# A rank update stacked on chip for the first batch, and other edits at the edges of a conditioned residual layer

## The chip, the cores and the metric

One core of a Trainium2 chip runs the kernel. The metric is the device time in microseconds, the median of several runs. Times inside a profile are microseconds from the first instruction of one profiled execution.

## The reference

For each of 32 batches, x is 512 rows by 512 features, and f is 512 features by rank 16, used on both sides:

```
z1 = einsum('bfi,bir->bfr', x, f) / 512
z  = einsum('bfr,bor->bfo', z1, f) / 16
y  = einsum('bfi,oi->bfo', x, W) + fc_bias + z + cond
out = x + gelu(y, approximate=False)
```

All of it is fp32. Since z = x (f f^T) / 8192, the layer of batch b is x times one matrix of its own, full_w = W + f f^T / 8192.

## The kernel before

Everything is held transposed: features on partitions in four chunks of 128, rows along the free dimension. For each batch TensorE forms the update f f^T in PSUM (`update`), VectorE adds it, scaled, to the base weights (`full_w`, L335), and TensorE multiplies full_w with x.

fp32 precision comes from splits. ScalarE copies a tile to the shorter fp32r type (`w_high`, L263; `x_high`, L257), VectorE subtracts that from the whole (`w_low`, `x_low`, L331), and three products are summed in PSUM: high with high, high with low, low with high. The factors are split the same way, for four batches (a group) at a time: `f_parts` holds 64 rows, 16 for each batch, as high, low and whole. From it SP copies five pieces by DMA (`stack_factors`, L175) into `f_stack`: high, high, low, low on one side against high, low, high, low on the other, 16 rows each, so that one product over 64 rows gives the update with all four terms. From batch 2 on the stack is written twice, on rows 0 to 63 and 64 to 127, and products over 64 rows are put alternately on the two halves of the array (`halves`, L457, 96 products of a batch), four phases of two output tiles each. Batches 0 and 31 use whole 128-row products (`piece` L481, and the end of `step` L576). Batch 1's update uses rows 0 to 63 only (`in_whole`, L163). `f_stack` has two buffers, used by odd and by even batches.

Batch 0 is special (`piecewise`, L127). Its factors are loaded straight to the last 16 of 128 rows of `f_first`, the other rows being zeroed, and its update is four full-precision fp32 products (`first_update`, L518): two before the first piece and one after each of the next groups of four. It is then worked off chunk by chunk: update, full_w, splits, products. Batch 1's update is put into PE's queue inside batch 0's third piece (L513), and batch 2's update at the head of batch 1's step (L568). The order on every engine is the order of the program text.

SP's queue issues all DMAs in one order: the factors of batch 0, x and weights in chunks, the factors of group 0, x of batch 1, the biases; then, behind a wait for the split factors of group 0, stack 1 (five DMAs), the factors of all other groups in one load of 896 KB, stack 2 (ten DMAs), x of batch 2. In the step of batch b it issues stack b + 3 after the update of batch b + 1, in the first step also x of batch 3, then the two stores of the batch, then x of batch b + 4. ScalarE in step b takes the last GELUs of batch b - 1, the splits of batch b + 1, the first GELUs of b. A half product of a new batch waits until the GELU has read its bank.

The last batch finishes its four output tiles one after another; the last tile is one GELU, one addition of x and one store, both stores of it by SP.

## Time and profile before

| what | us |
| --- | --- |
| three runs | 380.54, 381.37, 382.89 (median 381.37) |
| profiled execution, its time | 380.12 |
| its span, first to last instruction | 378.3 |
| PE busy | 371.0 (98%) |
| DVE (VectorE) busy | 296.7 (78%) |
| ACT (ScalarE) busy | 203.8 (54%) |
| chain that ended last | PE 93%, SP's queue 3%, DMA 2%, DVE 1% |
| granted TensorE clock | 1.000 over the span |

The chain that ended last is followed back from the last instruction, at each step to what released it. PE is TensorE's products, PEld its weight loads, SPq the issuing of DMAs by SyncE. The time "to landing" of a DMA runs from its issue. Matmuls are pipelined, so their records overlap, and a name of a line can be that of a helper.

### The profile page before, as it was taken

To read this page: it belongs to the slowest core of one execution; us is meant where nothing else is said; L and a number is where in the kernel's file an instruction comes from. 1 tells how busy PE (TensorE), PEld (TensorE's weight loads), DVE (VectorE), ACT (ScalarE), POOL (GpSimd) and SP (SyncE) were. 2 spreads that over 40 slices of the span, in tenths; PEclk is the share of its full clock that TensorE was granted. 3 is DMA by queue.
4 is the path that set the end of the run, shared out by engine and by line. 5 is a ranking of instruction groups with operands and counts; after the bars stand their busy time and mean duration, and the time that the engine had idled before them with its cause. 6 is when DMAs were issued, how large, how long until landed. Compare 5 with 4: busy or idle time off the path is not lost.

```text
span 378.3 us, 7900 instructions
## 1 busy us (share of the span) xinstructions
PE 371.0 (98%) x3111; PEld 302.0 (80%) x3111; DVE 296.7 (78%) x182; ACT 203.8 (54%) x209; POOL 0.7 (0%) x5
## 2 busy tenths in 40 slices
PE   8989999999999999999999999999999999999995
PEld 4768888888888888888888888888888888888874
DVE  5699788887788877788877878878778987778932
ACT  5385445665455565545565446575445665446531
POOL 0000000000000000000000000000000000000000
PEclk9999999999999999999999999999999999999999
DMA  7999887678786778787678886777887777883222
GB/s 242 258 248 334 280 269 230 204 234 246 217 267 223 204 233 243 220 264 231 194 231 246 233 251 229 204 233 236 241 244 233 202 235 231 244 243 124 113 113 112
DMA packets 27565, 85.50 MB, mean 226 GB/s; under 512 B 6752, under 2 KB 6880, under 8 KB 23584
## 3 DMA queue, kind: packets, MB, share of 16 engines
q1 hardware_dynamic: 27552, 85.32, 73.5%
q8 instruction: 9, 0.15, 0.2%
q14 instruction: 4, 0.03, 0.0%
HBM read 35.75 MB, written 33.55 MB: 183 GB/s over the span
## 4 chain that ended last, share of the span: by engine, by line
PE 93%; SPq 3%; DMA 2%; DVE 1%; issue 0%; ACT 0%; DVEq 0%
PE y L454 86%; PE update L538 4%; SPq L186 2%; DMA f_stack<-f_parts 1%; PE y L438 1%; PE y L446 1%; PE y L442 1%; DMA base_w<-w_t 1%; DVE full_w L335 0%; SPq L206 0%; ACT result L293 0%; DVE result L385 0%; DVE f_parts L331 0%; DVE w_low L331 0%; DVE x_low L331 0%
## 5 line engine op out<-in xcount | busy, mean ns | idle before, releaser
L454 PE MATMUL y<-x_high,w_high 64*128 64x512 f32 x960 | 186.9, 386 | 0.0
L454 PE MATMUL y<-x_low,w_high 64*128 64x512 f32 x960 | 186.9, 386 | 0.0
L293 ACT ACTIVATE result<-y,bias 128x512 f32<-128x512 f32 x128 | 81.2, 686 | 159.1 <-PE y L454 151.3
L454 PE MATMUL y<-x_high,w_low 64*128 64x512 f32 x960 | 128.3, 386 | 0.0
L385 DVE TENSOR_TENSOR result<-result,x_in 128x1024 f32<-128x1024 f32 (+1 forms) x65 | 78.3, 1204 | 55.7 <-ACT result L293 55.7
L454 PEld LDWEIGHTS y<-x_low,w_high 64*128 64x128 f32 x960 | 89.9, 184 | 18.9
L454 PEld LDWEIGHTS y<-x_high,w_high 64*128 64x128 f32 x960 | 89.9, 184 | 18.9
L454 PEld LDWEIGHTS y<-x_high,w_low 64*128 64x128 f32 x960 | 89.9, 184 | 18.9
L335 DVE SCALAR_TENSOR_TENSOR full_w<-update,base_w 128x2048 f32<-128x2048 f32 (+2 forms) x36 | 73.9, 2054 | 21.6 <-PE update L538 18.6
L331 DVE TENSOR_TENSOR w_low<-full_w,w_high 128x2048 fp32r<-128x2048 f32 (+1 forms) x35 | 73.5, 2101 | 0.3
L331 DVE TENSOR_TENSOR x_low<-x_in,x_high 128x2048 fp32r<-128x2048 f32 (+1 forms) x35 | 73.5, 2100 | 0.0
L263 ACT ACTIVATE w_high<-full_w 128x2048 fp32r<-128x2048 f32 x31 | 59.4, 1915 | 4.6 <-DVE full_w L335 4.6
L257 ACT ACTIVATE x_high<-x_in 128x2048 fp32r<-128x2048 f32 x31 | 59.4, 1916 | 1.2 <-DMA x_in<-x_t 1.2
L538 PE MATMUL update<-f_stack 64*128 64x512 f32 x124 | 19.8, 389 | 1.6 <-DMA f_stack<-f_parts 1.6
L538 PEld LDWEIGHTS update<-f_stack 64*128 64x128 f32 x124 | 11.8, 184 | 4.8 <-DMA f_stack<-f_parts 2.1
L438 PE MATMUL y<-x_high,w_high 128*128 128x512 f32 x32 | 11.9, 418 | 0.0
L442 PE MATMUL y<-x_low,w_high 128*128 128x512 f32 x32 | 11.4, 403 | 0.0
L446 PE MATMUL y<-x_high,w_low 128*128 128x512 f32 x32 | 9.6, 406 | 0.0
L438 PEld LDWEIGHTS y<-x_high,w_high 128*128 128x128 f32 x32 | 6.4, 199 | 2.7 <-issue 1.4
L446 PEld LDWEIGHTS y<-x_high,w_low 128*128 128x128 f32 x32 | 5.9, 188 | 2.0 <-issue 0.6
L442 PEld LDWEIGHTS y<-x_low,w_high 128*128 128x128 f32 x32 | 6.0, 188 | 1.6 <-issue 0.5
L520 PE MATMUL update<-f_first 128*128 128x512 f32 x8 | 5.8, 843 | 0.0
(18 smaller groups left out, 22.9 us busy)
## 6 DMA issues: line engine op xcount, KB each, us to landing
out_t<-result SPq DMA_DIRECT2D x63, 512.0 KB, 3.4
x_in<-x_t SPq DMA_DIRECT2D x31, 1024.0 KB, 6.2
f_stack<-f_parts SPq DMA_DIRECT2D x183, 64.0 KB, 4.2
f_stack<-f_parts SPq DMA_DIRECT2D x122, 32.0 KB, 4.4
x_in<-x_first SPq DMA_DIRECT2D x4, 256.0 KB, 4.1
base_w<-w_t SPq DMA_DIRECT2D x4, 256.0 KB, 4.3
f_parts<-factors SPq DMA_DIRECT2D x1, 896.0 KB, 8.8
out_t<-result SPq DMA_DIRECT2D x2, 256.0 KB, 2.5
```

What stands on the lines that cost most here:

```text
L186: sp.dma_start(f_stack[slot][row + g * RANK:row + (g + 1) * RANK, sides, :].bitcast(fp32), pair).then_inc(stacked[slot], 16)
L257: nc.scalar.activation(x_high[j % SLOTS][:, :, :], x_in[j][:, :, :], ACT.Copy).then_inc(x_high_ready, 1)
L263: nc.scalar.activation(w_high[j % SLOTS][:, :, :], full_w[:, :, :], ACT.Copy).then_inc(w_high_ready, 1)
L293: nc.scalar.activation(result[j % SLOTS][:, m, :], y[m][:, :], ACT.Gelu, bias=bias[:, bass.ds(b * CHUNKS + m, 1)]).then_inc(gelu_ready, 1)
L331: nc.vector.tensor_tensor(out, whole, high.bitcast(fp32), ALU.subtract).then_inc(ready, 1)
L335: nc.vector.scalar_tensor_tensor(full_w[:, chunks, start:stop], update[:, chunks, start:stop], UPDATE_SCALE, base_w[:, chunks, start:stop] ...
L385: nc.vector.tensor_tensor(part, part, x_in[j][:, chunks, :], ALU.add).then_inc(result_ready, 1)
L438: nc.tensor.matmul(y[m][:, :], w_high[slot][:, c, m * P:(m + 1) * P], x_high[slot][:, c, :], start=(c == 0), stop=False)
L442: nc.tensor.matmul(y[m][:, :], w_high[slot][:, c, m * P:(m + 1) * P], x_low[slot][:, c, :], start=False, stop=False)
L446: mm = nc.tensor.matmul(y[m][:, :], w_low[slot][:, c, m * P:(m + 1) * P], x_high[slot][:, c, :], start=False, stop=(c == CHUNKS - 1))
L454: return nc.tensor.matmul(y[m][:, :], w[rows, c, m * P:(m + 1) * P], x[rows, c, :], start=first, stop=last)
L538: mm = nc.tensor.matmul(update[:, c, :], f_stack[slot][rows, 0, c * P:(c + 1) * P], f_stack[slot][rows, 1, :], start=True, stop=True)
```

## The change

It does the following.
- The 16 factor rows of batch 0 are loaded four times, to 64 rows (`f_first`). ScalarE makes the high part in two halves of 256 columns. VectorE makes each side of the stack as whole - high x mask, where the mask of a row is 1 on the rows that are to hold low parts; the masks come from a row number (GpSimd's iota), a bitwise and, and a multiplication. Rows 64 to 127 of both stacks are zeroed once.
- The updates of batches 0 and 1 are single fp32r products over 128 rows. The third and fourth of batch 0 now both stand behind the first group of high products.
- SP loads group 1's factors alone (128 KB), waits for batch 0's updates before stack 2 (the same buffer now holds batch 0's stack), and loads groups 2 to 7 (768 KB) in the first step, ahead of x of batch 3.
- The last output tile is finished in two halves of 256 columns; the second half is stored by ScalarE's queue.
- PE makes 8 idle products at the start instead of 3.

```diff
--- before.py
+++ after.py
@@ -31,6 +31,7 @@
 def cond_residual_kernel(nc, x_t, x_first, w_t, factors, cond, fc_bias, out_t):
     fp32 = mybir.dt.float32
     fp32r = mybir.dt.float32r
+    int32 = mybir.dt.int32
     ALU = mybir.AluOpType
     ACT = mybir.ActivationFunctionType
 
@@ -46,9 +47,12 @@
     PART_DMAS = 5
     HALF = CHUNKS // 2
     PIECEWISE = 1
-    WARM_UPS = 3
+    WARM_UPS = 8
     EDGE = FEATURES // 2
 
+
+    EDGES = [slice(n * EDGE, (n + 1) * EDGE) for n in range(2)]
+    LAST_PARTS = [(slice(CHUNKS - 1, CHUNKS), cols) for cols in EDGES]
 
     PHASES = ((0, 1), (2, 3), (1, 0), (3, 2))
 
@@ -73,7 +77,11 @@
         result = [sb(f"result{s}", [P, CHUNKS, ROWS], fp32) for s in range(SLOTS)]
 
 
-        f_first = sb("f_first", [P, FEATURES], fp32)
+        f_first = sb("f_first", [TILE, FEATURES], fp32)
+        f_first_high = sb("f_first_high", [TILE, FEATURES], fp32r)
+        rows = sb("rows", [TILE, 1], int32)
+        row_bit = sb("row_bit", [TILE, 2], int32)
+        low_rows = sb("low_rows", [TILE, 2], fp32)
         f_parts = sb("f_parts", [UNROLL * RANK, GROUPS, 3, FEATURES], fp32)
 
 
@@ -89,16 +97,22 @@
         y = [ps(f"y{m}", [P, ROWS], fp32) for m in range(CHUNKS)]
 
         f_first_loaded = sem("f_first_loaded")
-        f_first_zeroed = sem("f_first_zeroed")
+        rows_numbered = sem("rows_numbered")
+        bits_ready = sem("bits_ready")
+        low_rows_ready = sem("low_rows_ready")
+        f_first_high_ready = sem("f_first_high_ready")
+        first_moving_stacked = sem("first_moving_stacked")
+        first_weights_stacked = sem("first_weights_stacked")
         edge_full_w_ready = sem("edge_full_w_ready")
         edge_w_high_ready = sem("edge_w_high_ready")
-        f_loaded = [sem("f_loaded_group0"), sem("f_loaded_rest")]
+        f_loaded = [sem("f_loaded_group0"), sem("f_loaded_group1"), sem("f_loaded_rest")]
         bias_loaded = sem("bias_loaded")
         w_loaded = [sem(f"w_loaded{c}") for c in range(CHUNKS)]
         x_first_loaded = [sem(f"x_first_loaded{c}") for c in range(CHUNKS)]
         x_loaded = [sem(f"x_loaded{s}") for s in range(X_SLOTS)]
         f_high_ready = sem("f_high_ready")
         f_low_ready = sem("f_low_ready")
+        stack_zeroed = sem("stack_zeroed")
         stacked = [sem(f"stacked{s}") for s in range(SLOTS)]
         bias_ready = sem("bias_ready")
         idle_zeroed = sem("idle_zeroed")
@@ -168,6 +182,11 @@
             engine.dma_start(x_in[j][:, :, :],
                              batch_chunks(x_t, UNROLL * t + j, slice(0, CHUNKS))).then_inc(x_loaded[j], 16)
 
+        def store(engine, t, j, part):
+            chunks, cols = part
+            engine.dma_start(batch_chunks(out_t, UNROLL * t + j, chunks)[:, :, cols],
+                             result[j % SLOTS][:, chunks, cols]).then_inc(stored[j % SLOTS], 16)
+
         block = ctx.enter_context(nc.Block())
 
         @block.sync
@@ -190,7 +209,8 @@
             def load_first_x(c):
                 sp.dma_start(x_in[0][:, c, :], x_first[c]).then_inc(x_first_loaded[c], 16)
 
-            sp.dma_start(f_first[P - RANK:P, :], factors[0:RANK, 0, :]).then_inc(f_first_loaded, 16)
+            sp.dma_start(f_first[:, :], factors[0:RANK, 0, :].rearrange("(a r) i -> a r i", a=1)
+                         .to_broadcast([TILE // RANK, RANK, FEATURES])).then_inc(f_first_loaded, 16)
             load_first_x(0)
             sp.dma_start(base_w[:, 0, :], w_t[0]).then_inc(w_loaded[0], 16)
             sp.dma_start(f_parts[:, 0, 2, :], factors[:, 0, :]).then_inc(f_loaded[0], 16)
@@ -203,7 +223,8 @@
 
             sp.wait_ge(f_low_ready, 1)
             stack_factors(0, 1)
-            sp.dma_start(f_parts[:, 1:GROUPS, 2, :], factors[:, 1:GROUPS, :]).then_inc(f_loaded[1], 16)
+            sp.dma_start(f_parts[:, 1, 2, :], factors[:, 1, :]).then_inc(f_loaded[1], 16)
+            sp.wait_ge(update_ready, made(0))
             stack_factors(0, 2)
             load_x(sp, 0, 2)
 
@@ -217,15 +238,16 @@
                     sp.wait_ge(update_ready, made(b + 1))
                     stack_factors(t3, j3)
                 if is_first(t, j):
+                    sp.dma_start(f_parts[:, 2:GROUPS, 2, :], factors[:, 2:GROUPS, :]).then_inc(f_loaded[2], 16)
                     load_x(sp, 0, 3)
-                parts = [slice(0, HALF), slice(HALF, CHUNKS)]
+                whole_row = slice(0, ROWS)
+                parts = [(slice(0, HALF), whole_row), (slice(HALF, CHUNKS), whole_row)]
                 if is_last(t, j):
-                    parts[1:] = [slice(m, m + 1) for m in range(HALF, CHUNKS)]
+                    parts[1:] = [(slice(m, m + 1), whole_row) for m in range(HALF, CHUNKS - 1)] + [LAST_PARTS[0]]
                 for n, part in enumerate(parts):
 
                     sp.wait_ge(result_ready, 2 * b + n + 1)
-                    sp.dma_start(batch_chunks(out_t, b, part),
-                                 result[j % SLOTS][:, part, :]).then_inc(stored[j % SLOTS], 16)
+                    store(sp, t, j, part)
                 if j == 0 and not last_group:
 
                     sp.wait_ge(f_low_ready, t + 2)
@@ -236,13 +258,13 @@
             groups(sp, step)
 
             sp.wait_ge(stored[0], 2 * 16 * BATCHES // SLOTS)
-            sp.wait_ge(stored[1], 2 * 16 * BATCHES // SLOTS + 16 * (HALF - 1))
+            sp.wait_ge(stored[1], 2 * 16 * BATCHES // SLOTS + 16 * HALF)
 
         @block.scalar
         def _(act):
             def split_factors(t):
 
-                act.wait_ge(f_loaded[0 if isinstance(t, int) and t == 0 else 1], 16)
+                act.wait_ge(f_loaded[t if isinstance(t, int) and t < 2 else 2], 16)
                 nc.scalar.activation(f_parts[:, bass.ds(t, 1), 0, :].bitcast(fp32r),
                                      f_parts[:, bass.ds(t, 1), 2, :], ACT.Copy).then_inc(f_high_ready, 1)
 
@@ -290,11 +312,18 @@
                     act.wait_ge(stored[j % SLOTS], 2 * 16 * (UNROLL // SLOTS * t + j // SLOTS))
                 if m == 0 and is_first(t, j):
                     act.wait_ge(bias_ready, 1)
-                nc.scalar.activation(result[j % SLOTS][:, m, :], y[m][:, :], ACT.Gelu,
-                                     bias=bias[:, bass.ds(b * CHUNKS + m, 1)]).then_inc(gelu_ready, 1)
+                columns = [slice(0, ROWS)]
+                if is_last(t, j) and m == CHUNKS - 1:
+                    columns = [cols for _, cols in LAST_PARTS]
+                for cols in columns:
+                    nc.scalar.activation(result[j % SLOTS][:, m, cols], y[m][:, cols], ACT.Gelu,
+                                         bias=bias[:, bass.ds(b * CHUNKS + m, 1)]).then_inc(gelu_ready, 1)
 
             act.wait_ge(idle_zeroed, 1)
             nc.scalar.activation(idle_gelu[:, :], idle[:, 0:1], ACT.Gelu)
+            act.wait_ge(f_first_loaded, 16)
+            for cols in EDGES:
+                nc.scalar.activation(f_first_high[:, cols], f_first[:, cols], ACT.Copy).then_inc(f_first_high_ready, 1)
             for c in range(CHUNKS):
                 high_pieces(0, c)
                 if c == 0:
@@ -325,6 +354,9 @@
 
             groups(act, step)
 
+            act.wait_ge(result_ready, 2 * BATCHES + 2)
+            store(act, GROUPS - 1, UNROLL - 1, LAST_PARTS[1])
+
         @block.vector
         def _(dve):
             def low_part(out, whole, high, ready):
@@ -357,6 +389,8 @@
                     dve.wait_ge(w_high_ready, n - CHUNKS)
                     dve.wait_ge(w_low_ready, n - CHUNKS)
                 full_weights(one, rest, FEATURES, full_w_ready)
+                if n == 1:
+                    stack_first(0, EDGES[1], first_weights_stacked)
 
             def low_pieces(b, c):
 
@@ -366,8 +400,30 @@
                 dve.wait_ge(w_high_ready, n)
                 low_part(w_low[b][:, one, :], full_w[:, one, :], w_high[b][:, one, :], w_low_ready)
 
-            nc.vector.memset(f_first[0:TILE, :], 0.0).then_inc(f_first_zeroed, 1)
-            nc.vector.memset(f_first[TILE:P - RANK, :], 0.0).then_inc(f_first_zeroed, 1)
+            for s in range(SLOTS):
+                nc.vector.memset(f_stack[s][TILE:P, :, :].bitcast(fp32), 0.0).then_inc(stack_zeroed, 1)
+
+            dve.wait_ge(rows_numbered, 1)
+            bits = (2 * RANK, RANK)
+            for side in range(2):
+                nc.vector.tensor_scalar(row_bit[:, side:side + 1], rows[:, :], bits[side], None,
+                                        ALU.bitwise_and).then_inc(bits_ready, 1)
+            dve.wait_ge(bits_ready, 2)
+            for side in range(2):
+                nc.vector.tensor_scalar(low_rows[:, side:side + 1], row_bit[:, side:side + 1], -1.0 / bits[side], None,
+                                        ALU.mult).then_inc(low_rows_ready, 1)
+
+            def stack_first(side, cols, ready):
+
+                nc.vector.scalar_tensor_tensor(f_stack[0][0:TILE, side, cols], f_first_high[:, cols].bitcast(fp32),
+                                               low_rows[:, side:side + 1], f_first[:, cols], ALU.mult,
+                                               ALU.add).then_inc(ready, 1)
+
+            dve.wait_ge(low_rows_ready, 2)
+            for n, cols in enumerate(EDGES):
+                dve.wait_ge(f_first_high_ready, n + 1)
+                stack_first(1, cols, first_moving_stacked)
+            stack_first(0, EDGES[0], first_weights_stacked)
             for c in range(CHUNKS):
                 full_piece(0, c)
                 low_pieces(0, c)
@@ -378,11 +434,11 @@
                                     fc_sb[:, :].rearrange("p (a m) -> p a m", a=1)
                                     .to_broadcast([P, BATCHES, CHUNKS]), ALU.add).then_inc(bias_ready, 1)
 
-            def add_x(t, j, chunks):
-
-                dve.wait_ge(gelu_ready, CHUNKS * (UNROLL * t + j) + chunks.stop)
-                part = result[j % SLOTS][:, chunks, :]
-                nc.vector.tensor_tensor(part, part, x_in[j][:, chunks, :], ALU.add).then_inc(result_ready, 1)
+            def add_x(t, j, chunks, cols=slice(0, ROWS)):
+
+                dve.wait_ge(gelu_ready, CHUNKS * (UNROLL * t + j) + chunks.stop + cols.start // EDGE)
+                part = result[j % SLOTS][:, chunks, cols]
+                nc.vector.tensor_tensor(part, part, x_in[j][:, chunks, cols], ALU.add).then_inc(result_ready, 1)
 
             def finish_previous(t, j):
 
@@ -424,12 +480,15 @@
                 add_x(t, j, slice(0, HALF))
 
             groups(dve, step)
-            for m in range(HALF, CHUNKS):
+            for m in range(HALF, CHUNKS - 1):
                 add_x(GROUPS - 1, UNROLL - 1, slice(m, m + 1))
+            for chunks, cols in LAST_PARTS:
+                add_x(GROUPS - 1, UNROLL - 1, chunks, cols)
 
         @block.gpsimd
         def _(pool):
             nc.gpsimd.memset(idle[:, :], 0.0).then_inc(idle_zeroed, 1)
+            nc.gpsimd.iota(rows[:, :], [[0, 1]], base=0, channel_multiplier=1).then_inc(rows_numbered, 1)
 
         @block.tensor
         def _(pe):
@@ -504,11 +563,10 @@
                     high_high(b, m, c)
                 if n == 1:
                     first_update(2)
+                    first_update(3)
                 pe.wait_ge(x_low_ready, n)
                 for m in range(CHUNKS):
                     high_low(b, m, c)
-                if n == 1:
-                    first_update(3)
                 if n == HALF + 1:
                     rank_update(0, 1)
                 pe.wait_ge(w_low_ready, n)
@@ -517,7 +575,8 @@
 
             def first_update(c):
 
-                nc.tensor.matmul(update[:, c, :], f_first[:, c * P:(c + 1) * P], f_first[:, :],
+                pe.wait_ge(first_weights_stacked, c // HALF + 1)
+                nc.tensor.matmul(update[:, c, :], f_stack[0][:, 0, c * P:(c + 1) * P], f_stack[0][:, 1, :],
                                  start=True, stop=True).then_inc(update_ready, 1)
 
             def rank_update(t, j):
@@ -534,7 +593,7 @@
                 for c in range(CHUNKS):
                     if piecewise(t, j):
                         pe.wait_ge(full_w_ready, made(b - 2) + c + 1)
-                    rows = half_rows(0 if in_whole(t, j) else c % TILES)
+                    rows = slice(0, P) if in_whole(t, j) else half_rows(c % TILES)
                     mm = nc.tensor.matmul(update[:, c, :], f_stack[slot][rows, 0, c * P:(c + 1) * P],
                                           f_stack[slot][rows, 1, :], start=True, stop=True)
                     if piecewise(t, j) or c == CHUNKS - 1:
@@ -544,8 +603,8 @@
             for _ in range(WARM_UPS):
                 nc.tensor.matmul(y[0][:, :], idle[:, 0:P], idle[:, :], start=True, stop=True)
 
-            pe.wait_ge(f_first_zeroed, 2)
-            pe.wait_ge(f_first_loaded, 16)
+            pe.wait_ge(stack_zeroed, SLOTS)
+            pe.wait_ge(first_moving_stacked, len(EDGES))
             first_update(0)
             first_update(1)
             for c in range(CHUNKS):
```

## Rows read from the trace of the kernel before

**Rows 1.** Chain that ended last, in order of time: start us, us, what

```profile
1.67 3.17 DMA base_w<-w_t
...
17.60 4.89 DMA f_stack<-f_parts
...
22.53 0.73 PE update L538 x4
...
34.17 0.45 PE update L538 x4
34.62 10.88 PE y L454 x96
```

**Rows 2.** Timeline, first 25 us: start us, us, engine, line, tiles, shapes, count [idle before]

```profile
0.74 0.52 POOL L432 MEMSET idle<- 128x512 bf16 x1 [0.29 <-POOLq L612]
0.75 0.41 SPq L193 DMA_DIRECT2D f_first<-factors  x1
0.91 0.48 DVE L369 MEMSET f_first<- 64x512 f32 x1 [0.91 <-PEq L612]
...
1.32 1.46 PE L545 MATMUL y<-idle 128*128 128x512 bf16 x3 [1.32 <-POOL idle L432]
...
2.83 3.75 PE L520 MATMUL update<-f_first 128*128 128x512 f32 x4
...
4.94 0.76 DVE L335 SCALAR_TENSOR_TENSOR full_w<-update,base_w 128x256 f32<-128x256 f32 x2 [2.90 <-PE update L520]
...
5.40 0.42 ACT L276 ACTIVATE w_high<-full_w 128x256 fp32r<-128x256 f32 x1 [0.92 <-DVE full_w L335]
...
5.96 1.82 PE L438 MATMUL y<-x_high,w_high 128*128 128x512 f32 x4
...
7.52 3.42 SPq L186 DMA_DIRECT2D f_stack<-f_parts  x5
...
15.82 1.20 PE L538 MATMUL update<-f_stack 64*128 64x512 f32 x4
...
17.05 2.29 DVE L335 SCALAR_TENSOR_TENSOR full_w<-update,base_w 128x2048 f32<-128x2048 f32 x1 [3.12 <-PE update L538]
...
19.38 1.92 ACT L263 ACTIVATE w_high<-full_w 128x2048 fp32r<-128x2048 f32 x1 [4.58 <-DVE full_w L335]
...
21.20 2.40 ACT L293 ACTIVATE result<-y,bias 128x512 f32<-128x512 f32 x4
```

**Rows 3.** Line L186 on SP: stack 1's issues and landing, then stack 3's landing

```profile
L186 SPq DMA_DIRECT2D f_stack<-f_parts x5: 590/655/752, 7.5 to 10.3; - x5
...
DMA to landing us min/median/max: 4.9/5.5/6.1
...
DMA to landing us min/median/max: 3.0/4.5/6.2
```

**Rows 4.** DMA issues, 0 to 30 us: size each, median us to landing

```profile
f_parts<-factors SPq DMA_DIRECT2D x1, 896.0 KB, 8.8
...
f_parts<-factors SPq DMA_DIRECT2D x1, 128.0 KB, 3.1
...
f_first<-factors SPq DMA_DIRECT2D x1, 32.0 KB, 1.9
```

**Rows 5.** x of batch 3: its issue, its landing, and ScalarE's split of it

```profile
25.47 0.58 SPq L168 DMA_DIRECT2D x_in<-x_t  x1
...
DMA to landing us min/median/max: 7.0/7.0/7.0
...
35.39 1.92 ACT L257 ACTIVATE x_high<-x_in 128x2048 fp32r<-128x2048 f32 x1
```

**Rows 6.** Timeline of the tail, and the last stores' row of the DMA issues

```profile
374.00 0.69 ACT L293 ACTIVATE result<-y,bias 128x512 f32<-128x512 f32 x1 [2.03 <-PE y L446]
374.71 0.69 DVE L385 TENSOR_TENSOR result<-result,x_in 128x512 f32<-128x512 f32 x1 [2.02 <-ACT result L293]
...
out_t<-result SPq DMA_DIRECT2D x2, 256.0 KB, 2.5
```

## The prediction

> **What bounds the kernel now.** I read the page's chain of waits first, then the chain in order of time, then the timeline of the first 25 us and of the last 6, then DMA landings. The chain by engine, on the page, is nearly all PE; the chain in order of time [rows 1] says which parts are not. One batch is four update products in 0.45 us and 96 half products in 10.88, together 11.33, and this pair repeats 29 times up to 362.83 without a gap between them. Nothing in the diff touches that loop: the shapes, the order and the count of its instructions stay. So only what lies before 22.9 (batch 1's first half product) and behind 374.0 (the last product) can move the time.
>
> Before 22.9 several chains run close together, and I need the one that ends last:
> - **Stack of batch 2.** Its last DMA is issued at 17.60 and lands 4.89 us later, at 22.49; PE's update follows at 22.53 [rows 1] and the first half product at about 22.87 (22.53 + 0.73 less the overlap of a 0.39 us product).
> - **ScalarE.** Batch 1's first half products open on banks that batch 0's GELUs 0 and 1 must free. The four GELUs start at 21.20 and take 2.40 in all [rows 2], steps of 0.57 with a last one of 0.69, so the second ends at 22.46. It is level with the stack: removing the stack's lateness alone gives only 22.87 - 22.46 = 0.4 us.
> - **What sets the GELUs.** They stand behind ScalarE's split of batch 1's weights (19.38, 1.92), behind VectorE's full_w (17.05, 2.29), behind the update products of batch 1 (15.82, 1.20) [rows 2]. Call the start of those products T. Before, T = 15.82, in PE's own order; the stack that they need had landed at 10.3 + 4.9 = 15.2 [rows 3]. That is the row to look at: PE can come at most 0.6 us sooner before that stack is the wait.
>
> **The change, part by part.**
>
> *Batch 0's update in single products.* Removed: 4 full-precision products, two records each; the first two products take 3.75 us for four records from 2.83 on, about 0.9 a record, and update 0 releases full_w at 4.94 [rows 2]. The weights for it land at 1.67 + 3.17 = 4.84 [rows 1], so there is nothing to win at this point even with a free update. Added ahead of it, one after the other: the load, now 64 rows and 128 KB for 32 KB; two ScalarE copies of 256 columns; three VectorE operations of 256 columns; then the product.
> - Load: bounded by the 32 KB row's 1.9 us and the 64-row 128 KB row's 3.1 us [rows 4]; I take 2.4, since that second row also queued behind 512 KB. It starts at 0.75 [rows 2] and lands at 3.15 (2.65 to 3.85).
> - ScalarE: 0.42 each [rows 2], two in a row overlapping by 0.1 as the GELUs do: 3.6 and 3.9.
> - VectorE before it: two memsets of 64x1024; the 64x512 one took 0.48 [rows 2], so 0.48 to 0.97 each, I take 0.97, nearest by elements: 0.91 to about 3.0. The four one-column operations have no row; between 0.1 (nothing but a step) and 0.3 each, I take 0.15: 3.6. The iota on GpSimd starts at 1.26 (0.74 + 0.52) and has until 3.0; its price is also unseen, from 0.1 to unknown; the nearest row is the 0.52 memset, and that is my value: hidden.
> - VectorE's three operations: 0.38 each (0.76 for two, [rows 2]): 4.0, 4.4, 4.75.
> - PE: 8 warm-ups instead of 3. Three took 1.46 [rows 2], a step of 0.42 and 0.6 for the last, so 8 end at 1.32 + 3.4 = 4.7, just under the 4.8 at which the data is there: nothing, at most 0.1. Then one weight load and one product, 0.6: update 0 ready at 5.4, full_w at 5.45 instead of 4.94, **0.5 later**.
> - Behind it VectorE has one more operation of 0.38 ahead of batch 0's splits. So the split factors are ready 0.9 later, and SP's first stack DMA, which waits for them, starts at 8.4 instead of 7.52 [rows 2].
> - PE gains: the third and fourth first products fall from two records to one, and the first group of four high products (5.96, 1.82 for four, [rows 2]), of which the first steps at 0.42, should run at the 0.227 step of the loop (10.88/48) since PE has then been busy much longer. 1.2 GHz is 0.427 for 512 columns, 2.4 GHz 0.213. Groups of four then take 0.91. With VectorE's pieces 2 us apart (three operations of a quarter of 2.29 and a little), PE opens the third piece at 12.5 and is ready for batch 1's update eight products later, at 14.3.
>
> *So T is now set by DMA.* The five DMAs of stack 1 are issued 0.9 later and still queue behind a megabyte of x; their landing is set by the bytes ahead, not by their issue (4.9 against the 3.0 of a stack that finds the queue free, [rows 3]). 96 KB more lie ahead: between 0 (they fit where the queue is still empty at the start) and 96/195 = 0.5 us, the rate at which 896 KB landed between 15.2 and 19.8 (issued behind the five at 10.3 + 0.65, landing 8.8 later) [rows 3, 4]. I take 0.2, as most of it falls into the queue's empty start: **T = 15.4**, 0.4 sooner than before.
>
> *Batch 1's update on 128 rows.* Four products of 0.227 and a last of 0.39 are 1.07 against 1.20: 0.13 sooner. full_w at 16.5 instead of 17.05, and everything on ScalarE and VectorE behind it 0.5 sooner: second GELU done at 21.95.
>
> *Group 1's factors alone.* 768 KB leave the queue ahead of stack 2: up to 3.9 us at 195 KB/us. Then the issue is the limit: the last DMA starts at 17.60 + 0.9 less about 0.2 for the smaller load = 18.3, and lands 3.0 later (the least of the ten behind it, [rows 3]) at 21.3; with update products 21.7. That is under 21.95, by 0.25 only. The new wait for batch 0's four updates passes near 8 and SP reaches it after 12: nothing. So batch 1's half products start at 22.0 instead of 22.87: **0.85 gained**.
>
> *The rest of the factors later.* 768 KB, 3.9 us of queue, now go ahead of batch 3's x, which was issued at 25.47 and took 7.0 [rows 5]. It would land at 33 to 37; ScalarE wants it at 35.39 [rows 5] less 0.85. Landing at 37 it gives x_high at 38.9 (1.92) and x_low at 41.2 (2.29), and PE wants that at 45.1 (34.62 + 11.33 - 0.85): nothing. If the cover were gone (landing after 40.8) it would cost one for one.
>
> *The tail.* Before: GELU 374.00 + 0.69, add 374.71 + 0.69, store of 256 KB landing 2.5 after issue [rows 6]. Now half GELUs 0.42 with a step of 0.34, second half's add of 0.38 done at 375.15: 0.25 sooner. The last store is 128 KB, at the rate above up to 0.65 less, but its other half travels beside it and its rows are half as long; it also goes out by ScalarE's queue, which no row shows. Between -0.3 and 1.0 for the whole tail; I take **0.5**.
>
> Sum against the profiled execution: 380.12 - 0.85 - 0.5 = 378.8. The runs' median, 381.37, lies 1.25 above it, and the same 1.35 off it gives **380.0**.
>
> **The rivals.**
> - *The broadcast load holds up the queue.* Its source has a slowest dimension of 4 (copies), where every other load here has 16 or more. If it then used 4 of the 16 engines, those carry 32 KB each, at 195/16 = 12 KB/us for an engine 2.6 us at most. What follows on those engines lags too, but the queue is not full before 5, and that rate is one of short rows; I put 1.0 of it on stack 1: T = 16.2, second GELU 22.7, stack 2 at 22.0 or so; start gains 0.15, tail 0.5: 380.7. Nothing in the trace speaks against it, as no such load is in it. The Trainium skill, DMA: Bandwidth & Descriptors, "Why a DMA increments its semaphore by 16 and not by 1", says that the number of engines is the largest up to 16 that divides both sides' slowest dimensions, which would be 4 here; at its 27 GiB/s for an engine the lag would be 1.1 us by estimate. Chance 0.27.
> - *The iota is late (slower than before).* VectorE can't mask before it. Up to 3.0 it is free; from there update 0 slips one for one. The start has 1.5 us to spare before batch 1 begins at 22.87 again (22.87 against 21.3 to 21.7 for the stack chain), and 0.5 more from the tail: it decides from an iota that ends at about 5.0, 3.7 us long. One of 6 us would end at 7.3: 4.3 later, 2.8 over, less 0.5: 383.7. For it: GpSimd ran only memsets here. Against it: the one over 512 columns took 0.52 [rows 2]. The Trainium skill, GPSIMD Engine Reference, "Instruction dispatch", gives about 6 us for the first call of a freshly loaded kernel; no row here shows one. Chance 0.10.
> - *The moved factors hurt.* x of batch 3 after 40.8, above: 382 and more. Chance 0.05.
> - *Stack 1 lands early after all*, say because the queue serves its small packets between x's: T = 14.3, 1.1 more, but then stack 2 binds at 21.3: gain 1.2 + 0.5 and a better tail: 379.2. Chance 0.08.
> - The forecast: 0.50.
>
> **The numbers.** Within the forecast the bounds are 1.35 ± 0.7 (T 0.3, tail 0.5, stack 2 0.3); the runs of one kernel spread by 2.3 us here, so a median of a few moves by some 0.8. Reaching to the first and fourth rival: 378.4 to 381.8. About 1%, 3.8 us, is what a measurement of this kernel can tell from no change. Faster than 377.6 needs more than the whole start gives: 0.03. Slower than 385.2 needs an iota of 8 us or a broken loop: 0.04. Same: 0.93.
>
> **What would show it.** Update 0 at 5.3 to 5.6; first stack DMA at 8.2 to 8.6; batch 1's update products at 15.4, with PE waiting for f_stack before them; stack 2 landed before the second GELU ends; batch 1's first half product at 22.0, released by ScalarE's GELU; the loop unchanged at 11.33; last add at 375.15. It is wrong if the first load lands after 4, if the iota ends after 3, if PE waits in batches 2 or 3, or if the update of batch 1 starts by PE's order.

## The result, and the profile after

| | us |
| --- | --- |
| changed kernel, median of 22 runs | 383.86 (383.39 to 384.40) |
| kernel before, median of 22 runs beside them | 381.99 (380.47 to 383.63) |
| ratio | 1.0055, 95% interval 1.0043 to 1.0067 |
| changed kernel, profiled execution and its span | 383.47 and 381.7 |

Slower by 1.9 us, where 380.0 and a range of 378.4 to 381.8 had been forecast. Three single runs far outside the rest (418.66 and 764.23 us of the kernel before, 538.96 us of the kernel with the small tiles last) are left out of all ratios.

The page of the changed kernel (span; engine, busy time and share; chain by engine):

```profile
span 381.7 us, 7920 instructions
PE 371.4 (97%) x3112; PEld 304.2 (80%) x3112; DVE 299.7 (79%) x191; ACT 204.7 (54%) x212; POOL 0.8 (0%) x6
...
PE 87%; SPq 7%; DMA 4%; DVE 1%; issue 1%; ACT 0%; DVEq 0%
```

TensorE's busy time is what it was (371.0), the span 3.4 us longer. The timeline of the changed kernel's start answers [rows 2]:

```profile
0.74 0.76 SPq L212 DMA_DIRECT2D f_first<-factors  x1
1.02 0.91 DVE L404 MEMSET f_stack<- 64x1024 f32 x1 [1.02 <-PEq L671]
1.29 0.12 POOL L491 IOTA rows<- 64x1 int32 x1
...
1.32 3.59 PE L604 MATMUL y<-idle 128*128 128x512 bf16 x8 [1.32 <-POOL idle L490]
...
5.56 0.72 ACT L326 ACTIVATE f_first_high<-f_first 64x256 fp32r<-64x256 f32 x2 [3.33 <-DMA f_first<-factors]
...
6.09 1.27 DVE L418 SCALAR_TENSOR_TENSOR f_stack<-f_first_high,low_rows,f_first 64x256 fp32r<-64x256 f32 x3 [2.62 <-ACT f_first_high L326]
...
7.51 0.70 PE L579 MATMUL update<-f_stack 128*128 128x512 f32 x2 [2.60 <-DVE f_stack L418]
...
8.02 0.76 DVE L367 SCALAR_TENSOR_TENSOR full_w<-update,base_w 128x256 f32<-128x256 f32 x2 [0.65 <-PE update L579]
...
9.03 2.04 PE L497 MATMUL y<-x_high,w_high 128*128 128x512 f32 x4 [0.82 <-ACT w_high L298]
...
10.99 3.35 SPq L205 DMA_DIRECT2D f_stack<-f_parts  x5
...
18.38 1.10 PE L597 MATMUL update<-f_stack 128*128 128x512 f32 x4
...
23.66 2.40 ACT L319 ACTIVATE result<-y,bias 128x512 f32<-128x512 f32 x4
```

Read down the starts. The mask is cheap: the iota takes 0.12 us and is long done, the memsets 0.91 each. But the first load, issued at 0.74, is what ScalarE waits for until 5.56; TensorE, out of idle products since 4.9, waits 2.60 us; full_w starts at 8.02 (4.94 before), the first stack DMA at 10.99 (7.52), batch 1's update at 18.38 (15.82) with no wait for its stack, the GELUs at 23.66 (21.20). Batch 1's first half product waits for the second GELU. First its line in the kernel before, then in the changed kernel:

```profile
23.10 0.39 PE L454 MATMUL y<-x_high,w_high 64*128 64x512 f32 x2
```

```profile
25.05 0.50 PE L513 MATMUL y<-x_high,w_high 64*128 64x512 f32 x2 [0.99 <-ACT result L319]
```

(The 22.87 of the prediction is where the last update product starts.) That is 1.95 of the 3.4 us. Two more parts are in the stretch that had been put down as untouched. The chain in order of time of the changed kernel answers [rows 1]:

```profile
48.09 0.74 PE update L597 x4
...
82.47 0.47 PE update L597 x4
82.93 10.90 PE y L513 x96
```

Batch 4's update starts at 48.09 behind a stack, in 0.74 us like a product pair that starts from a stall; and the loop's two pieces are 0.47 and 10.90 us, not 0.45 and 10.88: 11.367 a batch for 11.333, which is 1.0 us over the batches. The ten DMAs of that stack (line L205 on SP, its issues and their landing) took 9.5 us and more, where those of [rows 3] took 3.0 to 6.2:

```profile
L205 SPq DMA_DIRECT2D f_stack<-f_parts x10: 588/595/654, 32.3 to 38.2; - x10
...
DMA to landing us min/median/max: 9.5/11.0/12.7
```

The tail answers [rows 6]: last GELUs, last additions, ScalarE's store. The two last stores landed 2.0 and 2.1 us after their issue.

```profile
377.79 0.84 ACT L319 ACTIVATE result<-y,bias 128x256 f32<-128x256 f32 x2 [2.03 <-PE y L505]
378.30 0.79 DVE L441 TENSOR_TENSOR result<-result,x_in 128x256 f32<-128x256 f32 x2 [1.81 <-ACT result L319]
...
379.12 0.38 ACTq L187 DMA_DIRECT2D out_t<-result  x1
```

From the start of the last GELU to the end of the span it is 381.7 - 377.79 = 3.9 us, against 378.3 - 374.0 = 4.3: 0.4 gained. The sum: 2.0 (the start) + 0.8 (batch 4, sized below) + 1.0 (the loop) - 0.4 = 3.4, and the spans differ by 3.4.

The medians differ by 1.9 only. The profiled execution of before, 380.12, is 1.9 under its own median and under all 22 runs; that of the changed kernel is 0.4 under its own. The execution that I had built the forecast on was among the quickest of its kernel.

### The profile page after: what moved, and what is told of

It is laid out like the page before. It is cut to its first block, busy times and chain, and to the rows that moved or that the text cites. A ratio compares the mean times of both kernels' runs of the same rounds, so it can differ in the third digit from the quotient of the medians.

```text
span 381.7 us, 7920 instructions
## 1 busy us (share of the span) xinstructions
PE 371.4 (97%) x3112; PEld 304.2 (80%) x3112; DVE 299.7 (79%) x191; ACT 204.7 (54%) x212; POOL 0.8 (0%) x6
## 4 chain that ended last, share of the span: by engine, by line
PE 87%; SPq 7%; DMA 4%; DVE 1%; issue 1%; ACT 0%; DVEq 0%
PE y L513 80%; SPq L205 6%; PE update L597 4%; DMA f_stack<-f_parts 3%; DMA f_first<-factors 1%; PE y L497 1%; PE y L505 1%; PE y L501 1%; DVE f_stack L418 0%; SPq L182 0%; SPq L187 0%; DVE result L441 0%; DVE full_w L367 0%; SPq L241 0%; DVE f_parts L363 0%
## 5 line engine op out<-in xcount | busy, mean ns | idle before, releaser
L513 PEld LDWEIGHTS y<-x_high,w_low 64*128 64x128 f32 x960 | 90.6, 184 | 18.2
L597 PE MATMUL update<-f_stack 64*128 64x512 f32 (+1 forms) x124 | 20.3, 396 | 0.7 <-DMA f_stack<-f_parts 0.7
L597 PEld LDWEIGHTS update<-f_stack 64*128 64x128 f32 (+1 forms) x124 | 11.9, 184 | 3.9 <-DMA f_stack<-f_parts 1.5
L363 DVE TENSOR_TENSOR f_parts<-f_parts (+1 forms) x8 | 5.4, 676 | 0.0
```

The costliest lines, as they stand in the source:

```text
L363: nc.vector.tensor_tensor(out, whole, high.bitcast(fp32), ALU.subtract).then_inc(ready, 1)
L513: return nc.tensor.matmul(y[m][:, :], w[rows, c, m * P:(m + 1) * P], x[rows, c, :], start=first, stop=last)
L597: mm = nc.tensor.matmul(update[:, c, :], f_stack[slot][rows, 0, c * P:(c + 1) * P], f_stack[slot][rows, 1, :], start=True, stop=True)
```

## The experiments

Each ran beside the kernel before, on the same chip; ratios are to it, with 95% intervals. A ratio differs from the quotient of the two medians by up to 0.0025, so a difference of under 0.002 (0.8 us) between two kernels is not told by the time alone. "Stack b" is the factor stack of batch b, T the start of batch 1's update.

### The load over 16

```diff
-   factors[0:RANK, 0, :].rearrange("(a r) i -> a r i", a=1)
-                        .to_broadcast([TILE // RANK, RANK, FEATURES])
+   factors[0:RANK, 0, :].rearrange("r (a i) -> r a i", a=1)
+                        .to_broadcast([RANK, TILE // RANK, FEATURES])
-   bits = (2 * RANK, RANK)
+   bits = (2, 1)
```

> The changed kernel with the stack rows of batch 0 in another order: row 4r+a for factor row r and copy a, so that the load's source has 16 as its slowest dimension and not 4 (the masks take bits 2 and 1 of the row number, not 32 and 16). Theory 1 (the load of 128 KB ran on a quarter of the DMA engines and held up what follows on them): it lands about 2.4 us after its issue instead of 4.8, x and weights of the first piece land 1 to 2 us sooner, the first full_w is at 5.5 instead of 8.0, TensorE never idles over 1 us before batch 1, and the time falls by 2.0 to 2.8 us against the changed kernel, to between 0.998 and 1.001 of the kernel before. Rival 2 (128 KB into 64 rows from one 32 KB source costs this much, or four reads of the same rows do): the landing stays above 4 and the time stays at 1.0055 of before.

Measured: 382.95 us (7 runs), ratio 1.0041 (1.0021 to 1.0060); span 379.9. Its timeline:

```profile
3.71 0.72 ACT L326 ACTIVATE f_first_high<-f_first 64x256 fp32r<-64x256 f32 x2 [1.47 <-DMA f_first<-factors]
...
5.66 0.70 PE L579 MATMUL update<-f_stack 128*128 128x512 f32 x2 [1.00 <-DVE f_stack L418]
...
6.16 0.76 DVE L367 SCALAR_TENSOR_TENSOR full_w<-update,base_w 128x256 f32<-128x256 f32 x2 [0.65 <-PE update L579]
...
16.57 0.63 PE L597 MATMUL update<-f_stack 128*128 128x512 f32 x2
```

The same 128 KB, in another order of rows, lands at 3.69 and not at 5.54. The x and weights issued behind it landed 1.5 and 2.1 us sooner after their issue (2.9 and 3.1 us, in the changed kernel 4.4 and 5.2, in the kernel before 2.6 and 3.2). So the shape of the load, not its size, held up the queue, as theory 1 says; on how many engines it ran no row counts. About a microsecond of the landing is left (2.9 against 1.9 in [rows 4]); that the size or the longer issue makes it was not tried. The span fell by 1.8, a little under what I expected, the median by 0.9 only; the next run but one shows where the rest can go. Two more lines of this run, batch 1's first half product and batch 4's update:

```profile
23.25 0.51 PE L513 MATMUL y<-x_high,w_high 64*128 64x512 f32 x2 [1.06 <-ACT result L319]
...
46.33 0.73 PE L597 MATMUL update<-f_stack 64*128 64x512 f32 x4 [0.51 <-DMA f_stack<-f_parts]
```

The start is now only 0.15 later than before (23.10). Batch 4's stack is late all the same: its update comes 12.10 us after batch 3's, where the loop takes 11.37. With the loop's 1.0 and the tail's 0.4 that gives 0.15 + 0.8 + 1.0 - 0.4 = 1.6, the difference of the spans (379.9 and 378.3).

### The rest of the factors later

```diff
                 if is_first(t, j):
-                    sp.dma_start(f_parts[:, 2:GROUPS, 2, :], ...)
                     load_x(sp, 0, 3)
...
                     load_x(sp, t + 1, j)
+                if isinstance(t, int) and t == 0 and j == 2:
+                    sp.dma_start(f_parts[:, 2:GROUPS, 2, :], ...)
```

> The changed kernel with the 768 KB load of groups 2 to 7 moved from the first step, ahead of x of batch 3, to the third step, behind its load of x. Theory 1 (in the first step it filled the queue, so that the stack of batch 4 landed 9.9 us after its issue at 48.04, after TensorE wanted it): the update products of batch 4 start at about 47.4 instead of 48.09, with no wait for f_stack, the start of batch 1 stays at 25.05, and the time falls by 0.5 to 0.8 us. Rival 2 (the stack was late because SP issued it late, x and stores being as large as the factors): it is still waited for and the time stays.

Measured: 383.15 us (6 runs), ratio 1.0056 (1.0035 to 1.0076); span 380.7. The update of batch 4 (TensorE's timeline):

```profile
47.19 0.65 PE L598 MATMUL update<-f_stack 64*128 64x512 f32 x4
```

No wait, 0.65 us, 0.90 earlier than in the changed kernel, of which 0.2 is an earlier start of this execution: the stall was 0.7, and with it goes 0.1 by which the batch behind a stall takes longer (11.48 us). The trace shows theory 1; by the time alone the gain can't be told (0.7 by the medians, none by the ratios).

### Both

> Both edits together: load over 16 and the rest of the factors in the third step. If they are separate causes the gains add: 2.6 to 3.5 us under the changed kernel, 0.996 to 0.999 of before. If the lateness at batch 4 only came from the later start, this one equals the first within 0.3 us.

Measured: 382.08 us (12 runs), ratio 1.0003 (0.9984 to 1.0022); span 381.1. 1.8 under the changed kernel, less than expected, and still not faster than before. Its timeline and its chain have the reason:

```profile
7.57 2.05 PE L498 MATMUL y<-x_high,w_high 128*128 128x512 f32 x4 [0.63 <-ACT w_high L299]
```

```profile
12.21 6.22 DMA f_stack<-f_parts
...
18.46 1.20 PE update L598 x4
```

The first update is nearly as early as with the first edit alone (5.75 against 5.66), but T is 18.46, not 16.57. Two things are late at once. The four high products take 2.05 us (steps of 0.42 us for 512 columns, the level of 1.2 GHz), and TensorE's steps stay so up to 13.5; by its own order it would have come to batch 1's update at about 18.2. And the last DMA of stack 1 took 6.22 us to land, at 18.42, where with the first edit alone it had landed by 16.4. Either would have made T some 1.6 to 1.9 later, so this execution does not price the clock. Batch 4 has no stall here (11.37 us behind batch 3's update) and had one with the first edit alone: that stall does not come from the late start only, and the two causes are separate, as the first branch of the expectation had it.

### The change without the on-chip stack

The kernel before with these edits, 3 idle products and its full-precision first update kept:

```diff
+            nc.vector.memset(f_stack[1][TILE:P, :, :].bitcast(fp32), 0.0)
-                    rows = half_rows(0 if in_whole(t, j) else c % TILES)
+                    rows = slice(0, P) if in_whole(t, j) else half_rows(c % TILES)
-            sp.dma_start(f_parts[:, 1:GROUPS, 2, :], ...)
+            sp.dma_start(f_parts[:, 1, 2, :], ...)   # groups 2 to 7 in the first step
+            the last tile in halves, as in the change
```

> The kernel before (batch 0's update in full-precision products of f_first, 3 idle products) with the other three edits: group 1's factors alone and the rest in the first step, batch 1's update on 128 rows (rows 64 to 127 of stack 1 zeroed), the last tile in halves. Theory 1 (the on-chip stack's load is the whole loss): batch 1's update at 15.7 by TensorE's order, its first half product at 22.4 after the second GELU instead of 22.87, the last addition 0.2 sooner, so 0.5 to 1.0 us under before (0.997 to 0.999), less up to 0.7 if the stack of batch 4 is late here too. Rival 2 (one of these three also costs, the moved factors above all): at or above before.

Measured: 380.04 us (12 runs), ratio 0.9962 (0.9946 to 0.9979). More than expected, and 3.8 us under the changed kernel: everything that the change lost came with the on-chip stack, its small tiles among it. Batch 4's stack is not late here (update 11.33 us after that of batch 3, without a wait), although the 768 KB go at the same place. An early T is not the reason: the load over 16 had T = 16.57, here it is 16.71, and stack 4 was late there. What the traces show is how far SP is ahead of TensorE. It issued the last DMA of stack 4 at 38.2 in the changed kernel and at 36.9 with the load over 16, 9.2 and 8.7 us before TensorE's turn for batch 4's update, and it took 9.9 and 9.4 to land. Here it was at 36.0, 9.8 ahead, and took at most 9.1. The cover is thin in all three, and SP, whose first stack DMA waits for splits behind the on-chip stack (10.99, 9.14, here 8.01), had less of it with that stack. Whether anything else shortened it was not tried.

### Small tiles last

```diff
-        rows = sb("rows", [TILE, 1], int32)        # ahead of f_parts, f_stack
-        row_bit = sb("row_bit", [TILE, 2], int32)
-        low_rows = sb("low_rows", [TILE, 2], fp32)
+        the same three, after idle_gelu
```

> The changed kernel with the three small tiles (rows, row_bit, low_rows: 4, 8 and 8 bytes a partition) declared last and not ahead of f_parts and f_stack. In the changed kernel the loop's batch takes 11.367 us, in the kernel before 11.333: six pairs of products around each update step at 231 to 236 ns, not 227, which is 1.0 us over 29 batches. Theory 1 (f_stack stands at another address, off the boundary that TensorE or the DMAs read it fastest at): the batch falls to 11.333 and the time by 1.0 us. Rival 2 (it comes from the wait that the PE program meets in another phase, or from the queue): the batch stays at 11.367. Start and tail stay as in the changed kernel under both.

Measured: 382.82 us (11 runs), ratio 1.0032 (1.0016 to 1.0048): 1.0 less by the median, though the intervals of the two kernels' ratios overlap. The loop in its chain:

```profile
82.92 0.45 PE update L597 x4
83.37 10.88 PE y L513 x96
```

0.45 and 10.88: the batch is back at 11.333. The start was not as in the changed kernel, as I had expected it to be (T = 19.77, with TensorE's clock at half from 8.3 to 15.1), and batch 4's stack was in time (update 48.73, 11.33 behind batch 3's); so its profiled span gained 1.0 and 0.8, lost 1.4, and came out 0.4 shorter. This pair does price the clock: in both executions T comes by TensorE's own order, the first update 0.14 later here, and 6.8 us at half clock in place of 3.4 made T 1.39 later, so some 1.25 us for 3.4 us more.

### The kernel before, shifted

```diff
         f_first = sb("f_first", [P, FEATURES], fp32)
+        small = [sb(f"small{n}", [TILE, width], fp32) for n, width in enumerate((1, 2, 2))]
```

and a GpSimd memset of each at the start.

> The kernel before with three small tiles of 4, 8 and 8 bytes a partition declared between f_first and f_parts, and zeroed once by GpSimd. Theory 1 (addresses): the batch rises from 11.333 to 11.367 and the time by 1.0 us, 1.0026 of before. Rival 2 (the loop's rate has nothing to do with addresses): 11.333 and the same time.

Measured: 382.88 us (12 runs), ratio 1.0025 (1.0002 to 1.0047). Its loop:

```profile
91.89 0.47 PE update L541 x4
92.36 10.90 PE y L457 x96
```

0.47 and 10.90 again, now in the kernel before, by 20 bytes of tiles that nobody reads. Both directions agree: the place in memory of what follows them costs 0.034 us a batch. So do all fourteen kernels' traces: 11.37 us a batch in the five with small tiles ahead of `f_parts`, 11.33 in the nine without. In the records it is the update's two pairs of products and the three pairs behind them whose steps are 231 to 236 ns and not 227; which access is slow was not tried.

### The tail alone

The kernel before with the last tile in halves, as in the change.

> The kernel before with only the last output tile in halves, its second half stored by ScalarE's queue. All theories: the last addition ends 0.3 sooner, at 375.1 when the last product ends as before, and the span ends 0.4 to 0.5 us sooner; 0.9988 of before.

Measured: 381.36 us (12 runs), ratio 0.999 (0.9972 to 1.0009): as expected in size, not told from nothing by time. Last GELUs and last additions of its timeline:

```profile
375.58 0.84 ACT L304 ACTIVATE result<-y,bias 128x256 f32<-128x256 f32 x2 [2.03 <-PE y L462]
376.09 0.79 DVE L399 TENSOR_TENSOR result<-result,x_in 128x256 f32<-128x256 f32 x2 [1.81 <-ACT result L304]
```

Span end 379.5 less 375.58 is 3.9, against 4.3 before: 0.4. Its start, whose code is that of before, differs by more than the tail gains (batch 1's and batch 2's update):

```profile
17.21 1.43 PE L554 MATMUL update<-f_stack 64*128 64x512 f32 x4 [2.23 <-DMA f_stack<-f_parts]
...
24.12 0.73 PE L554 MATMUL update<-f_stack 64*128 64x512 f32 x4 [0.32 <-DMA f_stack<-f_parts]
```

Batch 1's update here waits 2.23 us for stack 1, until 17.21; in the shifted kernel, with the same start, it waited 1.14, until 16.49. In the profile that I forecast from it came at 15.82 without a wait. Behind the long wait TensorE's clock was also at half here, from 18.0 to 21.4. Batch 1's first half product came at 24.69, in the shifted kernel at 23.97, in the profile of the forecast at 23.10.

### Group 1 alone, the rest late

The kernel before with group 1's 128 KB in the old place and the other 768 KB in the third step.

> The kernel before with only group 1's factors loaded in the old place (128 KB, not 896 KB) and the rest in the third step behind its load of x. Theory 1 (in most executions of the kernel before the stack of batch 2 is what batch 1 waits for, and in the profiled one it happened to be early): 1.0 to 1.6 us less than before, 0.996 to 0.9975. Rival 2 (the GELU bound of the profile holds in all executions): 0.0 to 0.4 less.

Measured: 380.43 us (12 runs), ratio 0.9964 (0.9944 to 0.9983). Theory 1. Its timeline, batch 1's and batch 2's update, GELUs, first half product:

```profile
17.08 1.20 PE L540 MATMUL update<-f_stack 64*128 64x512 f32 x4 [1.47 <-DMA f_stack<-f_parts]
...
22.07 0.73 PE L540 MATMUL update<-f_stack 64*128 64x512 f32 x4
...
22.46 2.40 ACT L295 ACTIVATE result<-y,bias 128x512 f32<-128x512 f32 x4
...
23.85 0.50 PE L456 MATMUL y<-x_high,w_high 64*128 64x512 f32 x2 [1.05 <-ACT result L295]
```

Stack 1 is late here too (17.08), but batch 2's update no longer comes behind the GELUs: it is done before them, and batch 1 starts on the second GELU, at 23.85. Against the three profiles with the old load (23.10, 23.97, 24.69) that is 0.75 later, 0.1 and 0.8 sooner: the gain of 1.3 is shown by the times, and the traces of single executions bear it out in part only.

### All three repairs

The changed kernel with the load over 16, the rest in the third step, and the small tiles last.

> The changed kernel with three repairs: the load of batch 0's factors over 16, the load of groups 2 to 7 in the third step, the three small tiles declared last. Theory 1 (load, moved factors and addresses are separate and together with a slow clock the whole loss against the kernel without the on-chip stack): the batch takes 11.333, no wait for f_stack at batch 4, 1.0 less than with the first two repairs alone (382.1), so 381.1, 0.998 of before; still about 1 above the kernel without the on-chip stack, as TensorE stands idle for 1 us before its first update and for 1 us behind it and then runs at half clock for 3.4 us or more. Rival 2 (the on-chip stack is no loss once it is repaired): within 0.3 of 380.0.

Measured: 380.82 us (12 runs), ratio 0.9964 (0.9945 to 0.9984); span 378.8.

```profile
17.08 1.20 PE L598 MATMUL update<-f_stack 128*128 128x512 f32 x4 [1.59 <-DMA f_stack<-f_parts]
...
22.46 1.83 ACT L320 ACTIVATE result<-y,bias 128x512 f32<-128x512 f32 x3
23.86 0.50 PE L514 MATMUL y<-x_high,w_high 64*128 64x512 f32 x2 [1.29 <-ACT result L320]
```

Batch 11.333, no stall at batch 4, and batch 1's update waits 1.59 us for stack 1, as in the kernels without the on-chip stack. In microseconds this is nearest to theory 1's 381.1 and outside rival 2's 380.0 ± 0.3. But the kernel without the on-chip stack that ran beside it took 380.59, 0.2 less and not the 1 that theory 1 gave, and its ratio is 0.996: in what it says of the on-chip stack rival 2 holds. In this execution TensorE had short waits too (0.69 and 0.82, with the load over 16 alone 1.00 and 0.82) and its clock did not fall in the start. Repaired, the on-chip stack is neither a loss nor a gain that can be told.

### TensorE kept busy, and 3 idle products

The repaired kernel with 10 idle products at the start and 4 behind the second update:

```diff
+            for _ in range(4):
+                nc.tensor.matmul(y[0][:, :], idle[:, 0:P], idle[:, :], start=True, stop=True)
```

> The repaired kernel with 10 idle products at the start, not 8, and 4 more between batch 0's second update and its first group of products, so that TensorE has work from 1.3 to the first group without a gap of over 0.5. Theory 1 (the gaps are what lets the clock fall to half, 1.2 GHz, at 8 to 12 us): the clock stays at its full level from its first rise on, the first groups of four take 0.91 and not 1.7 to 2.0, batch 1's update starts 1 to 2 us sooner or waits for its stack at 15.5 to 17, and the time falls by 0.5 to 1.5. Rival 2 (the clock falls whatever TensorE did, or the start is set by DMA anyway): no change, or 0.2 more for the added products.

> The repaired kernel with 3 idle products at the start, as in the kernel before. Theory 1 (8 only fill the time to the first update and raise the clock sooner): TensorE is idle from 2.8 to 5.7, the clock is at half for longer, batch 1's update starts up to 1 us later, and the time is 0.2 to 1.0 more than with 8. Rival 2 (the warm-ups are worth nothing, since DMA or the later gaps decide): the same within 0.2.

Measured: filled 380.47 us (12 runs), 0.997 (0.9949 to 0.9991); with 3 idle products 381.05 (12 runs), 0.9974 (0.9955 to 0.9993). Two stretches of the changed kernel, then of the filled one, then of the repaired one that it should be compared with (the PEclk column, behind the busy times, is the granted clock):

```profile
4.00:8.00 4.00, 1.40 (x5) 0.30 (x3) 1.27 (x3) 1.24 (x3) 0.00 (x0) 1.00 0.86 259
8.00:12.00 4.00, 3.18 (x8) 2.42 (x8) 3.98 (x8) 2.20 (x5) 0.00 (x0) 0.61 1.08 410
```

```profile
4.00:8.00 4.00, 3.93 (x13) 1.51 (x12) 2.82 (x7) 2.26 (x6) 0.00 (x0) 1.00 0.75 245
8.00:12.00 4.00, 4.00 (x18) 3.11 (x17) 3.90 (x8) 1.86 (x4) 0.00 (x0) 1.00 1.05 414
```

```profile
4.00:8.00 4.00, 2.49 (x9) 1.08 (x8) 3.16 (x8) 1.83 (x6) 0.00 (x0) 1.00 0.82 225
8.00:12.00 4.00, 3.86 (x18) 2.90 (x17) 3.75 (x7) 2.33 (x5) 0.00 (x0) 1.00 1.05 406
```

The changed kernel had 1.40 us of products from 4 to 8 and ran at 0.61 of its clock from 8 to 12; the filled one had 3.93 and ran at 1.00. But the repaired one, with 2.49 and its waits left in, ran at 1.00 too. The first group of four took 1.16 us filled and 1.16 unfilled (at 7.12); with 3 idle products it took 2.04:

```profile
7.47 1.16 PE L498 MATMUL y<-x_high,w_high 128*128 128x512 f32 x4
...
16.06 1.20 PE L598 MATMUL update<-f_stack 128*128 128x512 f32 x4 [0.44 <-DMA f_stack<-f_parts]
```

```profile
7.46 2.04 PE L498 MATMUL y<-x_high,w_high 128*128 128x512 f32 x4 [0.63 <-ACT w_high L299]
```

So these runs do not show that the gaps let the clock fall: one execution without gaps and one with short gaps both kept it. In time neither edit does anything that can be told (0.35 us less and 0.23 more than the repaired kernel by the medians; by the ratios both are a little above it). The filled execution did come to batch 1's half products 1.0 us sooner (22.83 against 23.86), and gave 0.8 of it back at batch 6, whose stack, behind the 768 KB in the third step, was now late:

```profile
68.51 0.72 PE update L598 x4
```

That update came 12.02 us behind batch 5's, for 11.33. So the later place of the load does not always hide it either. The clock column shows 1.00 also where no change of the clock had yet been recorded: there only the steps of 0.42 us tell 1.2 GHz, with 3 idle products up to 11.4.

### The change without the on-chip stack, and the rest late

> The kernel before with group 1's factors alone and the rest in the third step, batch 1's update on 128 rows, and the last tile in halves: everything of the change but the on-chip stack and its warm-ups, and the moved load later. Both theories: 380.0 as the same with the moved load in the first step, or up to 0.4 less where that load still delayed a stack; 0.995 to 0.9965 of before, the fastest of all.

Measured: 380.59 us (12 runs), ratio 0.996 (0.9941 to 0.9979). Faster than both kernels, by 1.0 and 3.3 us by the medians, and not told from the run with the load in the first step (0.9962) or from group 1 alone (0.9964). The ratios of these three and of the repaired kernel lie within 0.0005 of each other, their medians within 0.8 us. What is common to the four is group 1's factors loaded alone.

## Why the prediction was wrong

- **The first load, "I take 2.4 ... lands at 3.15 (2.65 to 3.85)": the step that failed first.** It landed at 5.54, 4.8 us after its issue and outside the bounds, since both bounding rows were loads with 16 or more in their slowest dimension. The first rival had named the mechanism, and the load over 16 shows it; but it followed the lag through the queue only, to stack 1 (1.0 us, which on 15.4 makes T = 16.4, not the 16.2 that it has), not from the load itself through the update to SP's first stack DMA, which came 3.5 late, and gave 380.7. By the Trainium skill, DMA: Bandwidth & Descriptors, "Why a DMA increments its semaphore by 16 and not by 1", 4 engines would carry it. The runs agree in that the order alone takes 1.85 us off, more than the lag of 1.1 estimated from its figure; none of them counts the engines.
- **"So T is now set by DMA".** T was 18.38, in TensorE's own order, 2.6 later than before and 3.0 later than forecast, where I had TensorE ready at 14.3; stack 1 had landed at 17.0. I had let the first groups run at the loop's step "since PE has then been busy much longer". It had not: it stood for 2.6 us, then for 0.8, and its clock was at half from 8.8 to 12.3. So the late first link made T late twice, by the link itself and by up to 1.4 us (18.38 less 17.0) through the slow clock.
- **"Nothing" for the moved factors.** I followed x of batch 3, which was indeed hidden (ScalarE waited 0.8 us, nobody behind it). What was late was the next thing behind it in SP's queue, batch 4's stack: 0.8 us with what follows the stall. I had stopped at the first consumer behind the load and not followed the queue on. The cover is a matter of a few tenths: it held in the run without the on-chip stack and not with the load over 16, both with an early start.
- **"Nothing in the diff touches that loop".** True of its instructions, false of its data's addresses: 1.0 us, half of the loss by the medians.
- **The base.** All gaps were read from one execution that was 1.9 us quicker than the usual one. There stack 1 came with no wait; in other executions of the same start it is 0.7 to 1.4 us later. So group 1 alone, priced within the 0.85, is worth 1.2 to 1.4 against the usual execution. In the same execution batch 1's first half product was read at 22.87 and stands at 23.10, which made the forecast gain some 0.2 too small.
- **A sum:** 8 idle products at the step of 0.42 and 0.6 for the last are 3.54 us, not 3.4, and took 3.59; the late load hid it.
- **Right:** the iota rival did not happen (0.12 us); memsets, mask and stack operations about as priced; the GELU as the bound of batch 1's start; the tail (0.4 against 0.5). No run tried the wait before stack 2 or the 128-row update by itself.

So, against the quick execution of before: the on-chip stack's load with the clock behind it 2.0, batch 4's stack 0.8, the addresses 1.0, less 0.4 for the tail. Against the usual execution, which is 1.9 slower, 1.9 is left, since there group 1's factors also gain.

Open: why the steps at the update depend on the address, which part of the start's 2.0 us is the clock's, and why the clock fell in some executions and not in others with nearly the same gaps (the load over 16 alone against the three repairs).

## What to carry to other kernels

Price a DMA by the slowest dimension of both its sides before its bytes, and put the copies of a broadcast inside, not outside. Declare small tiles after the large ones and measure both: here 20 bytes ahead of the loop's operands cost 1.0 us. A diff that leaves the loop's instructions alone can still slow it. Behind a moved load, follow the queue to the last consumer that has little cover, not to the first. Before forecasting a start of a few microseconds, ask of each link how much it varies between executions: where DMAs queue behind one another, one profile is one draw.

## What the runs showed of the hardware that was not expected

- 20 bytes of tiles a partition ahead of the loop's operands changed the steps of the update's products and the three pairs behind them from 227 to 231 to 236 ns, in both directions of the test.
- The same 128 KB from 32 KB of rows landed in 4.8 us with 4 copies outermost and in 2.9 with 16 rows outermost, and the two loads of 256 KB behind it took 1.5 and 2.1 us longer.
- With 3.4 us more at half clock in the start (6.8 against 3.4 us, small tiles last against the changed kernel), batch 1's update came 1.25 us later. The first group of four products took 1.16 us in some executions and 2.04 in others.
- In executions with the same start, batch 1's update came at 15.82, 16.49 and 17.21, the later two behind the landing of its stack.
